# Attention operands padded with zero rows to 62 and 64 contraction rows, and the split of the last weights done wholly by GpSimd

## The reference

```
x = x + attention_a(layernorm(x))   # 32 heads of 16, rotary positions, keys and values from a latent of 64, no mask
x = x + ffn(layernorm(x))           # x @ W.T + bias + a mix of 8 low-rank terms
x = x + attention_b(layernorm(x))   # 32 heads of 16, causal, ALiBi slopes, bias on q, k, v and on the output
x = x + ffn(layernorm(x))           # the same weights again
```

## Time and profile before

| | us |
|---|---|
| median of three executions | 1858.4 |
| the profiled execution | 1866.97 |
| its span, first to last instruction | 1865.1 |
| PE busy in the span | 1744.0 |
| DVE busy | 1366.6 |
| ACT busy | 987.7 |
| POOL busy | 119.7 |

### The profile page before, as it was taken

One profiled execution on the slowest core, in us unless ns is written; L12 is line 12 of the kernel. 1 busy time (PEld: TensorE's weight loads), 2 busy tenths in 40 slices (PEclk: granted clock), 3 DMA queues, 4 the chain that ended last, 5 costly groups with the idle time before them and its releaser, 6 DMA issues. The chain is left out here.

```text
span 1865.1 us, 35240 instructions
## 1 busy us (share of the span) xinstructions
PE 1744.0 (94%) x14412; PEld 904.9 (49%) x14412; DVE 1366.6 (73%) x2495; ACT 987.7 (53%) x1169; POOL 119.7 (6%) x218
## 2 busy tenths in 40 slices
PE   6997999999999999999799998899999999999697
PEld 4553433333333333333347677555555555543486
DVE  3765799999999999996464542588787878762485
ACT  3332277777777777778301111056666666655210
POOL 3323000000000000000010000100000000002000
PEclk9998799999999999999899999999999999975699
DMA  7768304332333333321524246815445444511221
GB/s 212 211 190 213 63 15 87 65 70 53 53 53 56 53 53 53 64 46 58 149 64 135 69 115 208 160 28 107 81 80 89 72 84 77 87 30 56 83 85 68
DMA packets 116865, 167.67 MB, mean 90 GB/s; under 512 B 20828, under 2 KB 58092, under 8 KB 116588
## 3 DMA queue, kind: packets, MB, share of 16 engines
q1 hardware_dynamic: 114880, 160.11, 38.1%
q0 software_dynamic: 1824, 5.31, 1.6%
HBM read 100.34 MB, written 64.50 MB: 88 GB/s over the span
## 5 line engine op out<-in xcount | busy, mean ns | idle before, releaser
L513 DVE TENSOR_REDUCE a_mxp<-a_ps_m 128x1 f32<-128x512 f32 x1024 | 634.2, 683 | 48.3 <-PE a_ps_m L377 44.9
L492 ACT ACTIVATE a_p<-a_ps_s 128x1024 f32<-128x1024 f32 x512 | 522.4, 1025 | 170.6 <-PE a_ps_s L417 160.9
L513 DVE TENSOR_REDUCE b_mxp<-b_ps_m 128x1 f32<-128x512 f32 (+3 forms) x768 | 382.3, 551 | 116.8 <-PE b_ps_m L377 109.6
L492 ACT ACTIVATE b_p<-b_ps_s 128x1024 f32<-128x1024 f32 (+3 forms) x384 | 308.8, 810 | 231.3 <-PE b_ps_s L417 229.0
L377 PE MATMUL a_ps_m<-a_slot_qk 48*128 48x512 f32 x640 | 240.0, 452 | 0.9
L417 PE MATMUL a_ps_s<-a_slot_qk 50*128 50x512 f32 x640 | 233.1, 445 | 1.2
L436 PE MATMUL a_ps_o<-a_p,a_slot_v 128*32 128x256 f32 x2560 | 205.6, 390 | 10.0 <-ACT a_p L492 5.4
L417 PEld LDWEIGHTS a_ps_s<-a_slot_qk 50*128 50x128 f32 x640 | 96.4, 185 | 128.8 <-issue 122.7
L377 PE MATMUL a_ps_m<-slot_qk 48*128 48x512 f32 x384 | 145.7, 469 | 0.4
L417 PE MATMUL a_ps_s<-slot_qk 50*128 50x512 f32 x384 | 140.3, 466 | 2.2 <-DMA slot_qk<-a_cturned 1.6
L436 PE MATMUL a_ps_o<-a_p,slot_memory 128*32 128x256 f32 x1536 | 127.9, 403 | 7.3 <-ACT a_p L492 3.3
(11 more groups left out here) (166 smaller groups left out, 2453.7 us busy)
## 6 DMA issues: line engine op xcount, KB each, us to landing
va_groups<-w_o SPq DMA_DIRECT2D x16, 512.0 KB, 3.7
ka_parts<-pa_parts SPq DMA_DIRECT2D x16, 512.0 KB, 3.8
qa_parts<-pa_parts SPq DMA_DIRECT2D x32, 256.0 KB, 3.7
kb_parts<-slot_memory SPq DMA_DIRECT2D x16, 512.0 KB, 3.5
qb_parts<-slot_memory SPq DMA_DIRECT2D x32, 256.0 KB, 3.5
vb_groups<-w_proj SPq DMA_DIRECT2D x16, 512.0 KB, 3.2
a_slot_qk<-qa_parts SPq DMA_DIRECT2D x60, 128.0 KB, 4.5
a_slot_qk<-ka_parts SPq DMA_DIRECT2D x48, 128.0 KB, 6.9
```

What stands on the lines that cost most here:

```text
L492: act.activation(p_sb[:, (2 * u + pair) % NP, :, off:CHUNK], ps_s[:, 2 * pair:2 * pair + 2, off:CHUNK], ACT.Exp, scale=scale).then_inc(exp ...
L513: dve.tensor_reduce(to, from_, AX.X, ALU.max).then_inc(piece_taken, 1)
```

## The change

Each row tile of q and k is padded. Behind the head's own rows (48, or 50 with ALiBi) come zero rows up to row 62; the shift rows move from rows 48 and 49 (50 and 51) to rows 62 and 63. The maxima product contracts 62 rows and the score product 64, in both attentions. The zero rows are written once per slot and attention by DMA, from a DRAM tensor `zero_rows` that is itself copied from an input in `project_a`. A zero DMA writes 14 (b: 12) rows of 4096 float32, 229 KB (197 KB), over q and k together. In attention b the high parts of `w_proj` and `w_eff` are no longer made by ACT after step 13: POOL makes each just ahead of its low part.

```diff
         self.al = ALIBI_ROWS if biased else 0
-        self.crow = SROWS + self.al
-        self.rows = self.crow + SHIFT_ROWS
+        self.zero_row = SROWS + self.al
+        self.crow = ROW_TILE - SHIFT_ROWS
+        self.rows = ROW_TILE
+        self.qk = qk
...
             e.dma_start(self.k[row + self.crow:row + self.rows, :, :].bitcast(F32), ones).then_inc(done, 16)
+            e.dma_start(self.qk[row + self.zero_row:row + self.crow, :].bitcast(F32),
+                        zeros_d[0:self.crow - self.zero_row, :]).then_inc(done, 16)
             if self.al:
-                e.dma_start(self.q[row + SROWS:row + self.crow, :, :, :].rearrange("w a n t -> w (a n t)").bitcast(F32),
+                e.dma_start(self.q[row + SROWS:row + self.zero_row, :, :, :].rearrange("w a n t -> w (a n t)").bitcast(F32),
                             ones_d[:, :]).then_inc(done, 16)
...
-        own_rows = PAIR * (3 if self.al else 1)
+        own_rows = PAIR * (4 if self.al else 2)
...
-    SETS = 16 * (SLOTS - 1) * PAIR * (2 if causal else 1)
+    SETS = 16 * (SLOTS - 1) * PAIR * (3 if causal else 2)
...
             for n, (whole, high, low_part) in enumerate(to_split):
+                pool.tensor_copy(high[:, :, :], whole[:, :, :]).then_inc(w_high_ready, 1)
                 pool.wait_ge(w_high_ready, n + 1)
                 pool.tensor_tensor(low_part[:, :, :], whole[:, :, :], high[:, :, :].bitcast(F32),
                                    ALU.subtract).then_inc(w_split, 1)
...
                 step(s)
-                if s == NG - 3 and to_split:
-                    act.wait_ge(late_loaded, 16 * len(late))
-                    for whole, high, _ in to_split:
-                        act.activation(high[:, :, :], whole[:, :, :], ACT.Copy).then_inc(w_high_ready, 1)
...
                 (env["alibi"], env["ins"]["alibi"]),
+                (env["zeros"], env["ins"]["zeros"]),
```

More of the change, by code:

```diff
@@ L106, in load_v, with set_rows @@
                     ).then_inc(loaded, 16)
-    def set_rows(self, e, ones_d, done):
+    def set_rows(self, e, ones_d, zeros_d, done):
         ones = ones_d[:, :].rearrange("w (n t) -> w n t", t=S)
@@ L119, in count_loads, with load_share @@
         self.all_loaded = ctx.enter_context(nc.semaphore(f"{name}_loaded"))
-    def load_share(self, e, i, q_d, k_d, v_d, alibi_d, ones_d):
+    def load_share(self, e, i, q_d, k_d, v_d, alibi_d, ones_d, zeros_d):
         rows = len(Q_PARTS) * PAIR
@@ L130, in load_share @@
         else:
-            self.set_rows(e, ones_d, self.all_loaded)
+            self.set_rows(e, ones_d, zeros_d, self.all_loaded)
             if self.al:
@@ L135, in wait_loaded, with attention @@
     def wait_loaded(self, e):
-        own_rows = PAIR * (3 if self.al else 1)
+        own_rows = PAIR * (4 if self.al else 2)
         e.wait_ge(self.all_loaded, 16 * (PAIR * (len(Q_PARTS) + len(K_PARTS)) + 1 + own_rows))
-def attention(nc, tag, causal, scale, consts, q_d, k_d, v_d, o_d, z_d, alibi_d, ones_d, first, more, output, late, to_split):
+def attention(nc, tag, causal, scale, consts, q_d, k_d, v_d, o_d, z_d, alibi_d, ones_d, zeros_d, first, more, output, late, to_split):
     units = [(qh, kt) for qh in range(2) for kt in range((4 * (qh + 1)) if causal else 8)]
@@ L334, in _ @@
             for g in range(1, SLOTS):
-                slots[g].set_rows(sp, ones_d, rows_set)
+                slots[g].set_rows(sp, ones_d, zeros_d, rows_set)
             for g in range(1, SLOTS):
@@ L826, in _ @@
                             sp.wait_ge(late_loaded, 16 * (len(late) + 1))
-                        first.load_share(sp, i, env["qa_d"], env["ka_d"], env["va_d"], None, env["ones"])
+                        first.load_share(sp, i, env["qa_d"], env["ka_d"], env["va_d"], None, env["ones"],
+                                         env["zeros"])
                     if c == 0 and i == 0:
@@ L1251, in _ @@
                             first.load_share(sp, i, env["qb_d"], env["kb_d"], env["vb_d"],
-                                             env["alibi"], env["ones"])
+                                             env["alibi"], env["ones"], env["zeros"])
                     for t in range(TPC):
@@ L1464, in build @@
         "cos": ins["cos"], "sin": ins["sin"], "rot": ins["rot"], "ins": ins,
+        "zeros": nc.dram_tensor("zero_rows", [ROW_TILE - SHIFT_ROWS - SROWS, Slot.QK_WORDS], F32).ap(),
         "ones": nc.dram_tensor("ones_rows", [SHIFT_ROWS, GH // PAIR * S], F32).ap(),
@@ L1519, in build @@
             attention(nc, "a", False, DH ** -0.5, consts, env["qa_d"], env["ka_d"], env["va_d"],
-                      env["oa_d"], env["za_d"], None, env["ones"], first, [], output,
+                      env["oa_d"], env["za_d"], None, env["ones"], env["zeros"], first, [], output,
                       [(env["w"]["o"][:, :, :], env["Wo"].rearrange("(k p) n -> p k n", p=P))], [])
@@ L1528, in build @@
             attention(nc, "b", True, 1.0 / DH, consts, env["qb_d"], env["kb_d"], env["vb_d"],
-                      env["ob_d"], env["zb_d"], env["alibi"], env["ones"], first_b, [second_b], output,
+                      env["ob_d"], env["zb_d"], env["alibi"], env["ones"], env["zeros"], first_b, [second_b], output,
                       [(env["w"]["proj"][:, :, :], env["w_proj"].rearrange("(k p) n -> p k n", p=P))],
@@ L1569, in shape_constants @@
         "masks": masks.astype(np.dtype("bfloat16")),
+        "zeros": np.zeros((ROW_TILE - SHIFT_ROWS - SROWS, Slot.QK_WORDS), np.float32),
         "ones": np.ones((SHIFT_ROWS, GH // PAIR * S), np.float32),
```

## The result

The changed kernel takes 1853.42 us (median of 19 executions, 1838.08 to 1876.46), the kernel before 1862.96 us in the same job (median of 19). The ratio is 0.994, 95% interval 0.9921 to 0.996: faster by 0.6%. The ratios in this document leave out executions more than 1.5% above the fastest of their kernel; the medians hold them all. The prediction was 1831.6 us in a range of 1815 to 1850; it is wrong by 22 us. Some 4.6 of these come from its base: the three executions that it started from have a median of 1858.4, the 19 of this job one of 1862.96. As a change, -26.8 us was forecast and -9.5 measured. The sign is right, but of a gain of 29 us in one half of the change, 20 were lost again in the other.

What follows compares the result with a forecast made beforehand. PE sets the pace in attention b until ACT's two copies pause it and its clock falls to half. Terms -31.8 + 0 + 0 + 5 = -26.8 us, from the median 1858.4 to 1831.6 us, range 1815 to 1850.

Steps and rivals of the forecast that it cites:

- Part 1: Attention b, steps 14 and 15: without ACT's two copies PE has no pause and keeps full clock, -31.8 us (-33.0 to -27.9).
- Part 2: End of attention b: POOL's two casts, 3.0 us each (1.8 to 4.5), are covered by step 15, cost 0.
- the halved lead: POOL's start before the end of step 14: 5.3 us ahead in the profile, halved for the forecast, so at about 1675.
- Part 3: Wider row tiles on PE: as many instructions, weight loads of 185 to 191 ns beside the products, cost 0.
- rival A: Products over 62 and 64 rows bring the clock back sooner at the start of attention a: 7.3 us saved, 1824.3; chance 0.24.
- Part 4: Zero DMAs at the starts of both attentions and in `project_a` and mid: +5 us (1 to 15).
- Start of attention b: Zero DMAs of 0.79 MB there take 2.6 to 6.8 us, against 3.4 of slack: cost 0 (0 to 3.4).
- Rival D: Zero DMAs make attention b's shift rows late, PE pauses, the clock falls from step 0: up to 2090 us; chance 0.06.
- Slot 0: Its zero DMAs ahead of the stores of values in `project_a` and mid: 3 us for both (0 to 6).
- The wait at the start of a: Shift rows of attention a, for which PE already waits, come 2 us later (1.1 to 6.1) behind zero DMAs.
- B: The clock falls in step 15 of attention b, where PE waits for ACT: costs 11.8 us, 1843.4; chance 0.15.
- C: The clock falls all the same at or before step 14, by a pause only now showing: about 1860; chance 0.07.

Runs made afterwards that it cites:

- e1: The kernel before with only the high parts moved from ACT to POOL, no padding, no zero DMAs: 1832.24 us, ratio 0.9841.
- e10: The same kernel as e1, run again on another chip and day: 1834.29 us, ratio 0.9852.
- e5: e1 with the first shift rows of each attention issued by ACT's queue instead of SP's: 1840.3 us, ratio 0.9869.
- e3: The changed kernel with products over 48 to 52 rows; the zero DMAs stay, but write rows that no product reads: 1965.86 us.
- e4: The changed kernel with the first shift rows of each attention issued by ACT's queue instead of SP's: 1842.63 us, ratio 0.9909.
- e2: The changed kernel with the high parts made by ACT again after step 13; padding and zero DMAs stay: 1862.99 us, ratio 0.9996.
- e7: The changed kernel with maxima products over 48 and 50 rows as before, score products still over 64: 1856.16 us, ratio 0.9933.
- e8: e4 with the zero DMAs of slot 0 issued as the last DMAs of `project_a` and of mid: 1850.38 us, ratio 0.9923.
- e9: e1 with only the four zero DMAs of slot 0 added, among the stores, into rows that no product reads: 1843.86 us, ratio 0.9885.
- e6: e4 with slot 2's row DMAs issued behind the loads and the first half of the maxima: 1841.69 us, ratio 0.9894.

## Why the prediction was wrong

**Part 1, right.** Forecast -31.8 us; the profiles say -30.8 for the changed kernel (steps of 30.4 and 25.4 against 30.8 and 24.0 forecast) and 86.6 - 54.4 = -32.2 for e1. In medians it is -29.4 (e1) and -30.5 (e10 against its own before). That e1 and e10 (1832.2 and 1834.3) stand so near the 1831.6 that was predicted for the whole change is luck: for this part alone, from 1858.4, the working gives 1826.6. With ACT's copies gone, no clock falls in step 14 in any of the kernels, and in e1 and e10 none in step 15: that the copies brought the half clock of before is shown. In step 15 the clock can fall all the same (e5, e3).

**Part 2, right.** Two casts of 1.89 and 1.90 us, near the lower bound of 1.8, all of it hidden, 15 us to spare. POOL began 2.5 us ahead of the end of step 14, the halved lead of the working (which makes 1676.2 there, not the 1675 written). The Trainium skill (GPSIMD Engine Reference, 4.1 Engine selection) says that beside VectorE, GpSimd is roughly at line rate with one input and about twice as slow with two. The trace fits that, with 1.89 us for one input and 4.56 for two; no run here has the same operations on VectorE.

**Part 3, right as to duration** (185 ns per weight load, as before), and rival A takes up the rest.

**Part 4, the step that failed.** "Start of attention b: ... Cost 0 (0 to 3.4)." Two things were wrong in it. First, the delay: 6.6 us where the working had 2.6 to 6.8 and took an amount below the slack of 3.4. 0.79 MB in 6.6 us are 119 GB/s, the rate read at that very place (115), and not that of `project_a` (302). The estimate that only two busy engines get 64 KB more each (3.1 us, "just not late") was half of what was measured. Second and worse, a wait was priced by its length. The prediction's own rows say that 1.6 us of waiting at the start of a brings the clock down, so the upper end of that term wasn't 3.4 us but 3.4 us and a stretch at half clock behind them. Rival D had this price but was argued away with a sentence that its own numbers contradict: "even 115 GB/s make the delay no more than the slack", where 6.8 us stood against 3.4. It got 0.06. D's mechanism is what happened in the changed kernel (2.8 us, then 78 us at half clock in its profile), though not at D's price, and with the shift rows on another queue (e4) 9 to 11 us come back in the median. The waits of e2, e3, e7 and e8 for q of slot 1 (1.1, 3.6, 2.5, 3.1 us) show that the zero DMAs push a second thing past its time, which Part 4 didn't name: the loads that stand right behind them.

Slot 0 was the second mis-sized term: 3 us for both stages (0 to 6). e9 says 5.9 us at the start of b in the profile, the upper end of that range, and 9.6 in the median, with the noise said above. The transfers were priced by their bytes at 302 GB/s (1.5 and 1.3 us); what they cost is the wait of ACT and DVE for the stores queued behind them, 4.2 and 2.6 us longer. Both ends of the queue were tried (e8), and neither is free.

The wait at the start of a grew by 2.9 us in the profile (2 taken, 1.1 to 6.1).

In medians the padding with its DMAs took some 20 us (29.4 - 9.5), where the sum has 5 for Part 4 and an upper bound of 15.

**The rivals.** A came in part. Its sign was a clock back within 10 us at the start of a: it is down for 10 us there, where it was 24, but e1 without padding has 10 us too, so this alone tells nothing. What tells is e3 against the changed kernel: the same DMAs, and without the padding 112 us more in the median. The prediction gave A 0.24 as an alternative to the forecast; here it works together with D, and keeps it from costing the 255 us worked out for it. The time at half clock inside the attentions, us, from windows of 4 us over each profile:

| contraction | start of a | within b |
|---|---|---|
| 62 and 64 rows | 0 (e4), 3 (e2), 10 (after, e6, e8) | 78 and 3 (after), 20 and 3 (e2), 31 and 3 (e8), 0 (e4, e6) |
| scores 64, maxima 48 and 50 | 14 (e7) | 33 and 3 (e7) |
| 48 to 52 rows | 10 (e1), 17 (e5, e9, e10), 24 (before), 27 (e3) | 82 to its end (before), 393, 88 and 33 to its end (e3), 20 to its end (e5), 0 (e1, e9, e10) |

The Trainium skill (TensorE: Matmul & The Clock Gate, Part 1) ties the clock to how busy the PE has been and doesn't speak of rows. Here PE is 100% busy by the trace in the long stretches of b (78, 88 and 393 us), and behind like pauses the wide products come back sooner, most clearly behind ACT's copies (3 us in e2, 82 in before). But the stretches of one form vary by a factor of ten and more, and the pauses aren't the same. That width counts is shown by e3 and the changed kernel; how much it is worth behind a given pause is not, and what makes it is open. B was seen in e5 and e3, and for some 3 us in step 15 of the changed kernel, e7 and e8. C did not come.

**The sum.** In medians, each kernel taken from the kernel before in its own job: -30.5 us (e10); +9.6 for the zero DMAs of slot 0 (e9); +2.0 for the wide products together with the zero DMAs of slots 1 and 2, on a start of b that doesn't wait for shift rows (e4); +9.4 for the shift rows on SP's queue; together -9.5 (after). Each step is uncertain by some 5 us. The chances were too sure for the reason given in Part 4: 0.84 on faster than 1849.

The fastest version of all is the half of the change without padding, e1: 1832.2 us by the median, 1.6% below the kernel before. In e1 and in e10 one run in six is 98 and 43 us longer than the median, and by the mean e1 is behind: 1848.1, where e5 has 1839.6, e10 1842.0, e4 1843.7 and the changed kernel 1853.3. The kernels with padding lack such runs: none of the 70 of after, e2, e4, e6, e7 and e8 took over 1877 us, where the kernel before had 6 of 79 at 1885 or more, and e1, e3 and e9 had some too (e5 had none in six, e10 one of 1878).

## What to carry to other kernels

Price a wait of TensorE by what its clock does behind it, not by its length: here 2.8 us of waiting cost 31 more. Before a transfer is added at the head of a stage, find the small late one that everything waits for on the same queue, and try a queue of its own: at the start of attention b it took the wait away, at the start of a, with the engines busy to the last, it didn't in two profiles of three. And if the worked-out delay can exceed the slack at either bound, the consequence belongs in the range.

## What the hardware showed that was not expected

- The clock fell with PE busy for 2.00 of 2 us and no pause ahead of it in the trace (e3 at 1632), and then stayed down for 88 us.
- Waits of 1.2 us (e1 and e9, start of a) were enough for a fall; one of 0.8 us at the same place (e4, with 64 rows) was not. How long the clock stays down doesn't follow the wait: 1.2 us brought 10 us in e1 and 17 in e9, and in b 2.8 us brought 78 (after), 3.1 us 31 (e8), 3.6 us 393 (e3).
- Behind the same 3.8 us of copies on ACT, the clock was down for 3 us with 62 and 64 contraction rows and for 82 with 50 and 52.
- Products over 62 and 64 rows in place of 48 to 52, with the same DMAs, took the median from 1965.9 us (e3) to 1853.4 and the estimated time at half clock from 330 to 630 us (five of six executions) to 95 to 180.
- On ACT's otherwise empty queue, shift rows of 16 KB were back 5.3 us behind their issue in one profile (e4) and 10.4 and 10.8 us in two (e6, e8), with the DMA engines busy.
- SP's issue of one DMA took 5.82 us instead of 0.43 with the zero DMAs queued ahead of it.
- A one-input cast of 128x2048 numbers takes GpSimd as long as ScalarE: 1.89 and 1.90 us.
